# Ternary block in one piece with its norms by halves, its weights measured beside grouped attention, and latent attention on joined weights

## What is computed

```python
x = _layernorm(x + state_space_mixer(x))
x = _layernorm(x + fp8_grouped_attention(x, ctx_2048))   # 8 groups, 16 heads, self and cross
x = _layernorm(x + _L0_ffn_ref(x, w1, b1, w2, b2))       # ternary
x = _layernorm(x + _L1_attn_ref(x, wq, wkv_a, wkv_b, wo))  # latent attention
x = _layernorm(x + image_text_attention(x, ctx_2048))
x = _layernorm(x + gated_ternary_ffn(x))
```

```python
def _bit_quant(w):                                # w1 is 2048 x 512, w2 512 x 2048
    scale = jnp.maximum(jnp.mean(jnp.abs(w)), 1e-8)
    return jnp.clip(jnp.round(w / scale), -1.0, 1.0)
h = gelu(x @ w1q.T + b1); y = h @ w2q.T + b2      # exact gelu

q = (x @ wq).reshape(b, s, 16, 128 + 64); q_nope, q_pe = split(q)
ckv = x @ wkv_a; c, k_pe = ckv[..., :128], ckv[..., 128:]
q_pe, k_pe = rope(q_pe), rope(k_pe)
k_nope, v = split((c @ wkv_b).reshape(b, s, 16, 256))
scores = (q_nope @ k_nope.T + q_pe @ k_pe.T) / sqrt(192)   # causal
o = softmax(scores) @ v;  y = o.reshape(b, s, 2048) @ wo
```

## Time and profile before

| | |
|---|---|
| median of three runs | 2468.49 us |
| the profiled execution | 2475.73 us |
| its span | 2474.1 us |
| mean granted TensorE clock, as a share of 2.4 GHz | 0.954 |
| engine busy: PE, DVE, ACT, POOL | 91%, 59%, 47%, 19% |
| ternary block, from its first norm's matmul to the next block's first DMA | 1281.05 to 1448.76 |
| latent attention, from there to PE's last matmul | 1448.76 to 1909.4 |

### The profile page before, as it was taken

How to read it: one execution, slowest core, us unless ns; L and a number is a source line. 1 busy time by engine, 2 the same in 40 slices (tenths; PEclk the granted TensorE clock), 3 DMA queues, 4 the chain that set the end, 5 groups by cost and what they waited for, 6 DMA issues and landing times. The chain is left out here.

```text
span 2474.1 us, 37595 instructions
## 1 busy us (share of the span) xinstructions
PE 2248.6 (91%) x13708; PEld 1769.1 (72%) x13720; DVE 1464.5 (59%) x4001; ACT 1172.6 (47%) x2947; POOL 463.2 (19%) x380
## 2 busy tenths in 40 slices
PE   7998899999999999899965969999898697998998
PEld 4643788888888888788855945665656495665987
DVE  2275677777766777677756334454554256884534
ACT  1052657575756575667526324343433244773222
POOL 0220122222221222122200002223141100221433
PEclk9899999999999999999987979999999898999999
DMA  6001100000010000000020012213120510001300
GB/s 223 1 33 66 58 27 27 27 27 29 25 38 17 27 27 27 28 27 27 1 111 26 1 75 81 85 68 128 72 93 13 202 54 18 2 2 53 152 1 27
DMA packets 33683, 124.99 MB, mean 51 GB/s; under 512 B 4295, under 2 KB 14279, under 8 KB 28135
## 3 DMA queue, kind: packets, MB, share of 16 engines
q1 hardware_dynamic: 31208, 110.16, 12.1%
q0 software_dynamic: 2304, 12.58, 1.3%
HBM read 102.58 MB, written 20.15 MB: 50 GB/s over the span
## 5 line engine op out<-in xcount | busy, mean ns | idle before, releaser
L762 PE MATMUL psum<-qa_kv_raw,context 128*128 128x256 f32 (+1 forms) x1536 | 343.6, 380 | 0.0
L762 PEld LDWEIGHTS psum<-qa_kv_raw,context 128*128 128x128 f32 (+1 forms) x1536 | 277.2, 184 | 44.9
L748 PE MATMUL psum<-qa_w,qa_xq 128*100 128x256 bf16 (+1 forms) x3072 | 271.1, 249 | 18.7 <-issue 15.6
L748 PEld LDWEIGHTS psum<-qa_w,qa_xq 128*100 128x100 bf16 x3072 | 259.4, 127 | 20.7 <-issue 20.4
L864 ACT ACTIVATE qa_prob<-psum,qa_nm 100x361 f32<-100x361 f32 x128 | 72.0, 562 | 239.8 <-DVE qa_nm L981 239.8
L1749 PE MATMUL psum<-X,la_w_q 128*128 128x400 f32 x384 | 136.5, 508 | 8.1 <-DVE la_neg_swap L1907 7.7
L1073 POOL TENSOR_TENSOR qa_w<-qa_w_raw,qa_w 128x768 bf16<-128x768 f32 x32 | 52.7, 1646 | 448.4 <-DVE qa_w L923 448.4
L819 PE MATMUL psum<-qa_catq,qa_o 128*128 128x400 f32 x512 | 113.1, 364 | 9.9 <-DVE X L1020 6.0
L943 DVE BATCH_NORM_STATS2 qa_st<-psum 100x6 f32<-100x128 f32 x320 | 69.7, 285 | 88.3 <-PE psum L748 88.3
L2282 ACT ACTIVATE it_prob<-psum,it_nm 100x257 f32<-100x257 f32 (+1 forms) x256 | 101.9, 412 | 40.7 <-DVE it_nm L2306 40.7
L1749 PEld LDWEIGHTS psum<-X,la_w_q 128*128 128x128 f32 x384 | 74.3, 194 | 65.2 <-issue 14.0
(11 more groups left out here) (342 smaller groups left out, 5100.5 us busy)
## 6 DMA issues: line engine op xcount, KB each, us to landing
qa_w_raw<-in_qa_w SPq DMA_DIRECT2D x9, 1536.0 KB, 6.8
la_gf_raw<-in_gf_w SPq DMA_DIRECT2D x16, 768.0 KB, 4.2
gf_ternary<-gf_made POOLq DMA_DIRECT2D x16, 768.0 KB, 3.6
gf_w<-gf_ternary SPq DMA_DIRECT2D x4, 3072.0 KB, 25.5
qa_o_raw<-in_qa_o SPq DMA_DIRECT2D x8, 1024.0 KB, 4.9
la_w_q<-in_la_q SPq DMA_DIRECT2D x4, 1536.0 KB, 7.3
context<-in_context SPq DMA_DIRECT2D x8, 722.0 KB, 12.3
it_context<-in_context SPq DMA_DIRECT2D x8, 722.0 KB, 12.3
```

The costliest lines, as they stand in the source:

```text
L748: mm = pe.matmul(psum[0:T, 2 + at // 512, at % 512:at % 512 + width], xq[:, kind, k, b * T:(b + 1) * T], w3[:, s, part, k, at:at + width], ...
L762: mm = pe.matmul(psum[0:rows, i // 2, (i % 2) * 256:(i % 2) * 256 + 256], ctxT[:, k, b * TC + t0:b * TC + t0 + rows], kv_raw[:, s, k, :], ...
```

## The change

Three parts.

1. **Grouped attention.** The ternary weights stand a second time in DRAM, cut into 64 pieces of 128 x 256 (`ternary_pieces` on the host, a rearrangement alone; `TF_PIECE` = 256). In each of the 64 steps ACT waits for its piece, sums its magnitudes into one column of `abs_sums`, waits for that sum and issues the load of the piece after next on its own queue. `split_and_measure` is gone.
2. **Ternary block.** One block holds the norm ahead, the feed-forward and the norm behind, both with `HalfNorm`, whose `scale` is cut into `invert` and `apply`. Half 0 is normed and split first. POOL scales half 1 and makes its low parts; ACT's high parts of half 1 stand between chunks 4 to 7 of half 0; the norm of the result's half 0 stands between chunks of half 1 (mean after j = 1, variance after j = 4, roots after j = 7); the last half is normed by quarters at the end. All loops are straight code. Weights are loaded as quarters of both.
3. **Latent attention.** A head's keys are latents times w_k, so its scores are queries times w_k, transposed, times latents: for each head PE joins w_q and w_k (`join_keys`, four matmuls of 128 columns) and w_v and w_o (`join_values`, one of 512). ACT copies the joined weights out. The units "k" and "v" go, `scores` takes `lat` in place of kT, `weigh_values` takes the transposed latents `lat_s` for all four heads in one matmul, and the mask of four heads is added in one. Value joins stand in batches 0 to 3 of the group, the next group's key joins in batches 4 to 7; those of group 0 stand ahead of the loop, which runs over three groups, with the last as straight code. Two of the `magnitudes` move to batches 1 and 4. SP's loads follow this order.

```diff
@@ grouped_attention, ACT
+            def measure(g, s, b, n):
+                r = b % 2
+                act.wait_ge(piece_in[r], g * 64 + (16 * (b // 2) + 16))
+                here = slice(n, n + 1) if isinstance(n, int) else bass.ds(n, 1)
+                act.activation(size[:, :], piece[:, r, :], ACT.Abs, accum_out=abs_sums[:, here]).then_inc(S_["measured"], 1)
+                act.wait_ge(S_["measured"], n + 1)
+                load_piece(r, slice(n + 2, n + 3) if isinstance(n, int) else bass.ds(n + 2, 1))
             def step(g, s, b, n):
                 if not early(n, 1):
                     turned_out(n - 1)
+                measure(g, s, b, n)
                 if b < C:
                     scale_w(g + 1, 1 - s, b)
@@ ternary_ffn_stage, PE
+            nrm.mean(pe, 0)
+            pe.wait_ge(S_["totalled"], 2)
...
+            nrm.mean(pe, 1)
+            nrm.var(pe, 0)
+            nrm.var(pe, 1)
+            pe.wait_ge(S_["scale_ready"], 1)
+            for at in range(2):
+                pe.wait_ge(S_["part_lo"], at * C + C)
+                hidden(at, 0)
+                hidden(at, 1)
...
                 for j in range(FC):
+                    last = down(at, j)
                     if j + 2 < FC:
+                        hidden(at, j + 2)
+                    if at and j == 1:
+                        nrm.mean(pe, 2)
+                    if at and j == 4:
+                        nrm.var(pe, 2)
                 last.then_inc(S_["y_all"], 1)
+            pe.wait_ge(nrm.std_ready, 6)
+            keep_busy(2)
+            pe.wait_ge(S_["y_out"], 2 * C)
+            mean_of_last(0)
+            pe.wait_ge(S_["y_out"], 3 * C)
+            mean_of_last(1)
+            keep_busy(2)
+            nrm.var(pe, 3)
@@ DVE
+            for i in range(2):
+                nrm.scale(dve, 0, i)
+            ternary(0)
+            for c in range(C):
+                dve.wait_ge(S_["part_hi"], c + 1)
+                dve.tensor_tensor(parts[:, 1, c, half_of(0)], X[:, c, half_of(0)], parts[:, 0, c, half_of(0)],
+                                  ALU.subtract).then_inc(S_["part_lo"], 1)
+            for j in range(1, LEAD):
                 ternary(j)
+            for i in range(2):
+                nrm.invert(dve, 1, i)
@@ POOL
+            for i in range(2):
+                nrm.apply(pool, 1, i)
+            for c in range(C):
+                pool.wait_ge(S_["part_hi"], C + c + 1)
+                pool.tensor_tensor(parts[:, 1, c, half_of(1)], X[:, c, half_of(1)], parts[:, 0, c, half_of(1)],
+                                   ALU.subtract).then_inc(S_["part_lo"], 1)
@@ latent_attention_stage, PE
+                pe.matmul(psum[0:T, b % 2, 0:4 * T], ident_b[:, :], mask_b[:, :, :], start=True, stop=False,
+                          skip_group_check=True)
                 for h in range(4):
                     out = psum[0:T, b % 2, h * T:(h + 1) * T]
-                    pe.matmul(out, qT[:, h, tok], kT[:, h, tok], start=True, stop=False)
...
+                    pe.matmul(out, qT[:, h, tok], lat[:, tok], start=False, stop=False, skip_group_check=True)
...
+            def join_keys(h, done):
+                pe.wait_ge(S_["join_out"], done)
+                for k in range(C):
+                    mm = pe.matmul(psum[:, 6, k * LORA:(k + 1) * LORA], w_qt[:, h, k * P:(k + 1) * P], w_kt[:, h, :],
+                                   start=True, stop=True)
+                mm.then_inc(S_["join_mm"], 1)
+            def join_values(h, done):
+                pe.wait_ge(S_["join_out"], done)
+                pe.matmul(psum[:, 6, :], w_vt[:, h, :], w_o[:, h, :], start=True, stop=True).then_inc(S_["join_mm"], 1)
...
-                for h in range(4):
-                    mm = pe.matmul(psum[:, 4 + b % 2, h * T:(h + 1) * T], v[:, b, h * P:(h + 1) * P],
-                                   pT[:, b % 2, h, :], start=True, stop=True)
-                mm.then_inc(S_["o_mm"], 1)
+                pe.matmul(psum[:, 4 + b % 2, 0:4 * T], lat_s[:, b, :], pT[:, b % 2], start=True,
+                          stop=True).then_inc(S_["o_mm"], 1)
...
+                    if b < 4:
+                        join_values(b, g * 8 + b + 4)
+                    elif more:
+                        if b == 4:
+                            pe.wait_ge(S_["keys_in"], 32 * g + 64)
+                        join_keys(b - 4, g * 8 + b + 4)
+                    if b in sum_beside:
+                        magnitudes(g, *sum_beside[b], 7)
```

More of the change, by code:

```diff
@@ L1281, in _, with high_part @@
+                last.then_inc(S_["y_all"], 1)
+            pe.wait_ge(nrm.std_ready, 6)
[6 more added lines that the diff above has]
+            nrm.var(pe, 3)
         @block.scalar
         def _(act):
-            for half_at in range(2):
-                def chunk(j, m, r, ahead):
+            def high_part(at, c):
+                act.wait_ge(nrm.normed, 2 * at + 2)
+                act.activation(parts[:, 0, c, half_of(at)], X[:, c, half_of(at)], ACT.Copy).then_inc(S_["part_hi"], 1)
@@ L1285, in chunk @@
+            act.activation(spare[:, :], core.eps[1.0], ACT.Sqrt)
+            for u in range(2):
+                for i in range(2):
+                    nrm.square(act, u, i)
+            for u in range(2):
+                for i in range(2):
+                    nrm.root(act, u, i)
+            for c in range(C):
+                high_part(0, c)
+            for at in range(2):
+                for j in range(FC):
+                    m, r = at * FC + j, j % 2
                     act.wait_ge(S_["h_mm"], m + 1)
-                    bias = core.param("b1", j) if isinstance(j, int) else core.params[:, bass.ds(j + PARAM_AT["b1"], 1)]
@@ L1293, in _ @@
+                    if at and j in (3, 4):
+                        nrm.square(act, 2, j - 3)
+                    if at and j == 7:
+                        nrm.root(act, 2, 0)
+                        nrm.root(act, 2, 1)
+            for i in range(2):
+                nrm.square(act, 3, i)
+            for i in range(2):
+                nrm.root(act, 3, i)
         @block.vector
@@ L1318, in _ @@
[L1318 to L1332 removed]
+                    if not at and j + LEAD < FC:
+                        ternary(j + LEAD)
@@ L1623, in latent_attention_stage @@
             units += [("q", i, half), ("rot" if i < 2 else "swap", i % 2, half)]
-    for i in range(4):
-        for half in range(2):
-            units += [("k", i, half), ("v", None, 2 * i + half)]
-    takes_out = {"q": "act", "k": "act", "rot": "dve", "swap": "dve", "v": "dve"}
+    takes_out = {"q": "act", "rot": "dve", "swap": "dve"}
     RING = 6
@@ L1841, in _ @@
                 magnitude_and_sign(g, 3)
+            for h in range(4):
+                joined_keys(h, h)
+            act.activation(Y[:, :, :], X[:, :, :], ACT.Copy).then_inc(S_["copied"], 1)
+            with act.Fori(0, QUADS - 1) as g:
+                quad(g, True)
+            quad(QUADS - 1, False)
         @block.vector
```

376 lines of the change are left out of this document (198 added, 178 removed).

## The result

The changed kernel takes 2396.23 us in the median of four runs (2392.42 to 2400.9), the kernel before 2469.09 beside it: a ratio of 0.9705, interval 0.9681 to 0.9729, 73 us less. The forecast was 2394, with 2376 to 2422. The profiled execution took 2400.9 (span 2399.2), against 2401.6 forecast for it.

A forecast was written before the change was run, and what follows sets the result against it. PE, busy 91% of the span, bounds the kernel. Grouped attention +0.5, ternary block −25.6 and latent attention −49 make −74: the profiled 2475.73 becomes 2401.6, less 7.2 to the median, 2394 us, range 2376 to 2422.

The forecast's parts named there:

- the forecast 1.0: Grouped attention: measuring one weight piece costs ACT about 1.0 us a step, fitting into its 2.29 us idle; +0.5 us overall.
- its 1 us for each us, in each of 32 steps: Grouped attention: were ACT's idle cover gone, each microsecond too many a step would cost up to 32 us.
- Start: Ternary block: with the norm by halves, the first down product comes 22.3 us earlier.
- The term for POOL: Ternary block, half 0: POOL's six instructions block DVE instructions, costing 3.2 us, between 0 and 6.9.
- the 43.8: Ternary block, half 0: 15 pairs of PE steps (hidden and down product) at 2.92 us take 43.8 us.
- Half 1 and tail: Ternary block: half 1 +6.3 us from mean, variance and roots; tail after PE's end 13.7 us, so −8.9.
- The queries' stretch: Latent attention, each group of heads: projections to scores take 38.6 us instead of 53.1, −14.5.
- the saving of 2.8 on masks and value products: Latent attention, a group's eight batches: fewer masks save 0.15 us and fewer value products 0.2 us a batch, together −2.8.
- an overrun of ACT: Grouped attention: ACT is overrun and the kernel slower, 2479 us, 3%; milder at 3 us a piece, 2417 us, 4%.
- second rival: Ternary block: POOL and DVE exclude each other wholly, roots stall half 1; gain 18 instead of 25.6, 2402 us; 13%.
- The third: Latent attention: joins fill no waits and their narrow products cost more than priced, 2407 us; 12%.
- the fourth: Joins fill all waits and PE gets 2.4 GHz at latent attention's and the ternary block's heads, 2379 us; 8%.

The follow-up runs named there:

- The two directions (none, and nine times): The changed kernel without measuring weights in grouped attention: 2399.45 us, ratio 0.9711; with eight more sums of magnitudes in each of 64 steps: 2431.66 us, ratio 0.9855.

## Why the prediction was right

The time was within 2.3 us of the forecast, and that is partly luck: the table has misses of −2.0, +2.3 and +2.5 us in the parts, and the clock's −5.4 and +2.9 in unchanged code. The miss in latent attention is itself what is left of two larger ones.

**Grouped attention.** Right in mechanism and size: 1.08 us a piece of the forecast 1.0, covered. The two directions (none, and nine times) show the cover and its end. Beyond the cover its 1 us for each us, in each of 32 steps, was too much in the profile: 0.7 was paid.

**Start.** Right: 22.75 of 22.3. The gated block's start was a good row for it, since the same code runs there. What wasn't foreseen is the 1.2 GHz in it; it cost nothing: with PE kept busy the first down product came at 26.6.

**Half 0.** The term for POOL was right (3.0 of 3.2). The sum was wrong: −0.7 forecast, +1.6 measured. The step that failed is the 43.8, 15 pairs at PE's full pace from the first on. Without POOL's work half 0 still takes 46.2, 2.4 more than that. Of these 1.6 is the clock, for which the forecast has no term: the first two pairs take 4.40 and 3.09 instead of 2.92, without a wait of PE. With POOL idle:

```profile
1300.11 1.93 PE L1221 MATMUL psum<-tf_h,tf_w_down 128*128 128x400 f32 x8 [1.92 <-DVE tf_h L1355]
1301.84 2.87 PE L1212 MATMUL psum<-tf_parts,tf_w_up 128*128 128x400 f32 x8
1304.51 1.79 PE L1221 MATMUL psum<-tf_h,tf_w_down 128*128 128x400 f32 x8
```

The other 0.8 is at the end, where the last down product waits 0.4 for its low part with no hidden product left to fill. It was there before, too (0.40). The forecast put all 3.9 that half 0 had lost down to the table loads, but in the kernel before two steps with a load took 6.42 for 5.84:

```profile
1336.75 1.72 PE L1266 MATMUL psum<-tff_h,tff_w_down 128*128 128x400 f32 x8 [0.32 <-DVE tff_h L1311]
...
1343.17 1.72 PE L1266 MATMUL psum<-tff_h,tff_w_down 128*128 128x400 f32 x8 [0.32 <-DVE tff_h L1311]
```

That is 0.58 for each of the five loads after the first down product, 2.9 in all. (All six loads of the earlier trace rows start in or just before half 0, not over both halves.) The loads are gone, as forecast.

The clock and POOL overlap in the first pair. It takes 4.39 with POOL at work and the clock full (1311.41 − 1307.02, PE waits 1.21 for DVE), 4.40 with POOL idle and 1.2 GHz granted in part, and 5.5 in the changed kernel, which has both. So POOL's price depends on the clock beside it: 3.0 measured, and 3.8 at full clock (48.4 less 43.8 and 0.8, an estimate).

Of the rule of the Trainium skill, page "SBUF — State Buffer", section "Who interferes with whom", the traces here show more than the forecast took: DVE lost 5.6 of 6.9 us, near to a full exclusion. PE lost only half; that DVE makes its weights three chunks ahead and has 0.06 us a step to spare would explain it, which is argued, not shown.

**Half 1 and tail.** Right, +6.0 of 6.3 and −8.7 of −8.9. The two table loads around the roots are absorbed as said: behind them PE waits 0.55, of 0.9 forecast. How the tail's 13.8 divide was not measured.

**Latent attention.** The queries' stretch is right to 0.1 us in groups 2 to 4. In the first it gained 18.3 and not 14.5, since before the change its projections ran at a mean granted clock of 0.92; the forecast has no term for that. Scores and values are 3.6 us longer than before instead of 2.7, and this hides half of the miss: the row taken for before, 29.35, had a clock of 0.95. At 1.00, before:

```profile
1751.29:1779.76 28.47, 25.29 (x257) 24.21 (x257) 15.43 (x40) 17.20 (x74) 0.00 (x0) 1.00 0.00 0
```

So a full group pays 4.5 instead of 2.7 (32.97 − 28.47), and the last 1.5 instead of 1.0 (29.95 − 28.46). The step that failed there is the saving of 2.8 on masks and value products, 2.3 with the two magnitudes. Without joins the stretch is only 1.0 us shorter than before (27.51). PE's work in it is 2.2 less (23.12 for 25.29), as forecast, but 1.2 of that came back as time in which PE waits (4.4 for 3.2). The joins took 0.5 more than forecast: a key join is 0.92 (0.97 forecast) and a value join 0.89 (0.86), but 1.8 were filled and not 2.3. In all four groups, at the clocks of the profiled executions, this stretch missed the forecast by 6.7 us. The whole, −46.5 of −49, came near because the projections of the first group made up for 3.8 of them.

The rivals: an overrun of ACT is a real mechanism, seen here at 3.5 us a piece. Full exclusion (second rival) is near the truth for DVE and not for PE. The third and the fourth, joins that fill no waits and joins that fill all, are both wrong: 1.8 of 7.2 us are filled in a full group.

## What to carry over

A stretch without PE work closes when its work finds an engine that waits elsewhere: read that engine's idle time in front of what others wait for, price the moved step with all its issues, and the cover can be told to 0.1 us. When a wait is removed and nothing moves, look at the engine that feeds the next step, and there for short instructions with long times beside POOL. A gain of some microseconds has to be read in its own stretch and at equal granted clock, since the clock moves unchanged stretches by as much.

## What the chip showed that was not expected

- DVE's smallest instruction waits for POOL's whole one: 0.17 us became 1.60, 1.79 and 2.65 beside instructions of 3.08 and 3.09; in pieces of 512 columns it was 0.78 and 0.60. Reductions from PSUM beside the same instructions stayed at 0.57. The Trainium skill, page "SBUF — State Buffer", section "Who interferes with whom", says so of DVE's modes that use both ports; these rows agree with it, though none shows in which mode the instruction ran.
- The granted clock after the same idle stretch of 2.08 us was 1.00 in one kernel and 0.71 on average over 10 us in another, worth 4.3 us in a group of heads (95.7 and 100.0). The eight output projections of a group took 22.24 us at 1.00 and 23.93 at 0.93.
- ACT issues a DMA in 0.34 us, and its sum of magnitudes over 256 columns takes 0.42, with 0.20 for reading the sum.
